# A graph network's first aggregation pass: fp32 rows and weights, or scaled fp16 halves

## What is computed

```python
h = jnp.maximum(_layernorm(x, axis=-1), 0.0)
x = x + _L0_gnn_ref(h, L0_gnn_W, src, dst, edge_weight)
...
Z = jnp.matmul(X, W)
msg = Z[edge_src] * edge_vals[:, None]
agg = jax.ops.segment_sum(msg, edge_dst, num_segments=X.shape[0])
return jax.nn.relu(agg)
```

## Time and profile before

| | us |
|---|---|
| median of 3 runs (2910.2 to 2920.01) | 2912.24 |
| the profiled execution | 2933.06 |
| its span in the trace | 2931.8 |

### The profile page before, as it was taken

The page is one execution under the profiler, slowest core; times in us unless marked ns, Lnnn a source line. Parts: engine busy times, 40 slices in busy tenths (PEclk is TensorE's granted clock), DMA queues, the critical chain, the costliest instruction groups (busy, mean ns, idle before and its releaser), DMA issues.

```text
span 2931.8 us, 38669 instructions
## 1 busy us (share of the span) xinstructions
PE 2508.7 (86%) x9907; PEld 1397.3 (48%) x9907; DVE 1824.4 (62%) x4596; ACT 614.6 (21%) x1144; POOL 872.4 (30%) x900
## 2 busy tenths in 40 slices
PE   7888878868878888999989999998898598888886
PEld 5534444433333223666556556564787443333332
DVE  7765669668567775657333443334887387776666
ACT  4654420000046563000000000001665100000000
POOL 0366665666600000000000000000001466666665
PEclk9889998978976787999999999998999699999899
DMA  6685664555625444344711121111545466776665
GB/s 163 177 236 169 179 179 139 159 164 165 180 42 108 62 63 71 94 110 113 202 46 54 57 58 54 54 32 55 152 121 137 136 189 202 206 233 190 195 191 170
DMA packets 157069, 389.13 MB, mean 133 GB/s; under 512 B 44859, under 2 KB 46260, under 8 KB 156881
## 3 DMA queue, kind: packets, MB, share of 16 engines
q0 software_dynamic: 72400, 232.34, 27.6%
q1 hardware_dynamic: 83798, 153.04, 21.0%
q10 hardware_dynamic: 683, 1.28, 0.2%
HBM read 333.81 MB, written 52.72 MB: 132 GB/s over the span
## 4 chain that ended last, share of the span: by engine, by line
PE 56%; DVE 21%; issue 10%; DMA 6%; another core or an unknown queue 3%; POOL 3%; ACT 1%; SPq 1%; DVEq 0%; ACTq 0%
PE banks L2013 15%; PE banks L1876 15%; PE banks L1842 7%; PE banks L2007 7%; PE banks L2190 4%; DMA ring<-edge_counts 3%; POOL ring L2347 2%; DVE sel L1134 2%; DMA ring<-table,src_t 2%; DVE spare L1061 1%; DVE spare L1059 1%; PE banks L1831 1%; DVE rstd L898 1%; PE banks L2093 1%
## 5 line engine op out<-in xcount | busy, mean ns | idle before, releaser
L1876 PE MATMUL banks<-ring,sel 128*125 128x512 f32 x1682 | 893.1, 659 | 159.5 <-issue 98.4
L1876 PEld LDWEIGHTS banks<-ring,sel 128*125 128x125 f32 x1682 | 287.6, 199 | 476.7 <-issue 473.5
L2292 POOL DMA_INDIRECT ring<-table,src_t x440 | 435.1, 989 | 263.1 <-PE banks L1876 109.1
L2326 POOL DMA_INDIRECT x<-table,src_t x25 | 24.2, 966 | 1461.9 <-DMA x<-src_digits 1447.2
L2347 POOL DMA_INDIRECT ring<-table,src_t x401 | 385.7, 962 | 221.9 <-issue 94.3
L2013 PE MATMUL banks<-acc,ring 125*125 125x512 f16 x1900 | 438.2, 381 | 8.1 <-DVE ring L1262 6.6
L2013 PEld LDWEIGHTS banks<-acc,ring 125*125 125x125 f16 x1900 | 257.1, 137 | 161.9 <-issue 28.9
L1613 DVE TENSOR_TENSOR ring<-ring,banks 128x512 f32<-128x512 f32 x388 | 255.2, 684 | 121.7 <-DMA ring<-table,src_t 98.4
L2007 PE MATMUL banks<-spare 128*125 128x450 f16 x590 | 262.4, 508 | 52.8 <-DVE spare L1061 25.0
L1842 PE MATMUL banks<-wh,hTh 128*125 128x512 f32 x300 | 140.0, 467 | 71.0 <-DVE hTl L914 32.2
L2007 PEld LDWEIGHTS banks<-spare 128*125 128x125 f16 x590 | 92.5, 157 | 223.1 <-issue 221.3
(11 more groups left out here) (411 smaller groups left out, 3132.9 us busy)
## 6 DMA issues: line engine op xcount, KB each, us to landing
ring<-edge_counts SPq DMA_DIRECT2D x35, 683.6 KB
edge_counts<-big SPq DMA_DIRECT2D x175, 97.7 KB
ring<-table,src_t POOLq DMA_INDIRECT x841
sel<-edge_counts SPq DMA_DIRECT2D x11, 683.6 KB
acc<-dst_places SPq DMA_DIRECT2D x28, 256.0 KB
x<-dst_places SPq DMA_DIRECT2D x27, 256.0 KB
acc<-src_digits SPq DMA_DIRECT2D x28, 224.0 KB
x<-src_digits SPq DMA_DIRECT2D x27, 224.0 KB
```

Of the source, the lines that this page charges most:

```text
L1876: last = P.matmul(to, sel[:, n % SELS, :], rows, start=False, stop=True, skip_group_check=True)
L2292: G.indirect_dma_start(out=ring[:, i % RING, :], out_offset=None, in_=table[0][:, :], in_offset=bass.IndirectOffsetOnAxis(ap=src_t[:, i:i ...
```

## The change

`table[0]` becomes fp16 of twice the width: a row's high half, and the rest behind it, 2048 bytes as before. Both are scaled by a power of two, so that they fit fp16. The bound for it comes from the squares of W0 (ScalarE, one `Square` over 2048 columns; TensorE sums them over partitions; VectorE makes the powers in `row_scale`, turn 4). Each tile's product is now taken out twice: ScalarE writes the high half (`z_high`), VectorE the rest (`rows_rest(n - 6)`, behind `rows_low(n - 3)`), and this counts `pj_out`. VectorE's loop has one turn more.

The edge weights get a power of two of their own, from their maximum (VectorE in `step_tables`, TensorE at turns `TABLES_AT`, now 15, and `PEAK_AT`), and are split into two fp16 halves `w16`. A selection is made by one `scalar_tensor_tensor` for both halves, 2x125 columns of fp16 (`sel16`). A step is three fp16 matmuls: high weight by high row, high weight by rest, rest of the weight by high row. ScalarE undoes both scales as it takes a tile out. `zbuf` is replaced by `z_halves_at`, the same room as fp16; the counts of `below` that are waited for later move up by two.

```diff
@@ -111,7 +111,7 @@
     LATE = 4
-    TABLES_AT = 14
+    TABLES_AT, PEAK_AT, SCALES_AT = 15, 17, 300
     DEG_FROM = 46
...
@@ -615,6 +624,41 @@
+            def powers(n):
...
+            def row_scale():
+                V.wait_ge(w0_bound, 2)
+                own.mark(V.tensor_scalar(out=bound[:, 0:1], in0=bank[1][:, 0:1], scalar1=Z_NORM * Z_NORM, scalar2=1e-30, op0=ALU.mult, op1=ALU.max))
+                V.wait_ge(v_own, own.n)
...
+                powers(0)
+                V.tensor_copy(bound[:, 0:1], down[:, 0:1]).then_inc(w0_bound, 1)
+            def weight_scale():
+                V.wait_ge(below, 3)
+                own.mark(V.tensor_scalar(out=bound[:, 1:2], in0=bank[2][:, 128:129], scalar1=1e-30, scalar2=None, op0=ALU.max))
...
+                powers(1)
+                own.mark(V.tensor_tensor(unscale, up[:, 0:1], up[:, 1:2], ALU.mult))
+            def rows_rest(t):
+                V.wait_ge(z_high, t + 1)
+                V.scalar_tensor_tensor(out=z_halves_at(t)[:, D:2 * D], in0=bank[6 + t % 2][0:TN, :], scalar=down[0:TN, 0:1],
+                                       in1=z_halves_at(t)[:, 0:D], op0=ALU.mult, op1=ALU.subtract).then_inc(pj_out, 1)
+
             def iota_row(layer):
@@ -666,6 +710,13 @@
                 V.tensor_copy(dst_f.rearrange("p (c e) -> p c e", c=EC), ed[:, :, 1, :]).then_inc(consts, 1)
+                own.mark(V.memset(squares[:, 1:2], 0.0))
+                own.mark(V.scalar_tensor_tensor(out=dst_junk.rearrange("p (c e) -> p c e", c=EC), in0=edf[:, :, 2, :], scalar=-1.0,
+                                                in1=edf[:, :, 2, :], op0=ALU.mult, op1=ALU.max))
+                V.wait_ge(v_own, own.n)
+                own.mark(V.tensor_reduce(squares[0:EP, 1:2], dst_junk, axis=AX.X, op=ALU.max))
+                V.wait_ge(v_own, own.n)
+                yield
                 V.wait_ge(consts, 8)
@@ -698,6 +749,7 @@
                 V.wait_ge(below, 1)
+                V.tensor_reduce(peak, bank[2][0:1, 0:128], axis=AX.X, op=ALU.max).then_inc(below, 1)
                 own.mark(V.tensor_tensor(thr[:, :], bank[0][:, 0:TILES - 1], tile_f[:, :], ALU.add))
@@ -751,6 +803,7 @@
                 yield
+                weight_scale()
                 yield
@@ -767,7 +820,11 @@
                 V.tensor_copy(dl_t[:, :], bank[1][:, 0:STEPS]).then_inc(tables, 1)
-                V.tensor_copy(w_t[:, :], bank[2][:, 0:STEPS]).then_inc(tables, 1)
+                own.mark(V.tensor_scalar(out=scaled_w, in0=bank[2][:, 0:STEPS], scalar1=down[:, 1:2], scalar2=None, op0=ALU.mult))
+                V.wait_ge(v_own, own.n)
+                own.mark(V.tensor_copy(w16[:, :, 0], scaled_w))
+                V.wait_ge(v_own, own.n)
+                V.tensor_tensor(w16[:, :, 1], scaled_w, w16[:, :, 0], ALU.subtract).then_inc(tables, 1)
                 V.tensor_copy(tile_row[:, :], bank[3][0:1, 0:STEPS]).then_inc(tables, 1)
@@ -783,7 +840,7 @@
             beside = step_tables()
-            for n in range(TILES + 5):
+            for n in range(TILES + 6):
                 if 0 <= n - 1 < TILES:
@@ -792,6 +849,10 @@
                     rows_low(n - 3)
+                if n == 4:
+                    row_scale()
+                if 0 <= n - 6 < TILES:
+                    rows_rest(n - 6)
                 if n > 1:
...
@@ -1131,8 +1192,8 @@
                     V.wait_ge(stepped, step_value(i - SELS))
-                V.tensor_scalar(out=sel[:, i % SELS, :], in0=node_iota[:, :], scalar1=dl_t[:, i:i + 1],
-                                scalar2=w_t[:, i:i + 1], op0=ALU.is_equal, op1=ALU.mult).then_inc(sel_ok, 1)
+                V.scalar_tensor_tensor(out=sel16[:, i % SELS, :, :], in0=node_iota[:, None, :].to_broadcast([CE, 2, TN]), scalar=dl_t[:, i:i + 1],
+                                       in1=w16[:, i, :, None].to_broadcast([CE, 2, TN]), op0=ALU.is_equal, op1=ALU.mult).then_inc(sel_ok, 1)
                 if i == BEHIND - 1:
...
@@ -1736,6 +1797,7 @@
                     split_high(raw_w0)
+                    A.activation(square_junk, raw_w0.rearrange("p k d -> p (k d)"), ACT.Square, accum_out=squares[:, 0:1]).then_inc(w0_bound, 1)
                 t = n
@@ -1744,7 +1806,9 @@
                         wait_stored(A, TABLE_N + t - 3)
-                    A.copy(zbuf(t), bank[6 + t % 2][0:TN, :]).then_inc(pj_out, 1)
+                    if t == 0:
+                        A.wait_ge(w0_bound, 3)
+                    A.activation(z_halves_at(t)[:, 0:D], bank[6 + t % 2][0:TN, :], ACT.Copy, scale=down[0:TN, 0:1]).then_inc(z_high, 1)
@@ -1872,9 +1936,12 @@
                 to = tiles[0:TN, bass.ds(b, 1), :].rearrange("p a d -> p (a d)")
-                rows = ring[:, r, :] if layer < LAST else rows_at(i)
-                last = P.matmul(to, sel[:, n % SELS, :], rows, start=False, stop=True, skip_group_check=True)
-                if layer == LAST:
+                if layer < LAST:
+                    for a, half in ((0, 0), (0, 1), (1, 0)):
+                        last = P.matmul(to, sel16[:, n % SELS, a, :], ring16[:, r, half * D:(half + 1) * D], start=False, stop=True,
+                                        skip_group_check=True)
+                else:
+                    last = P.matmul(to, sel[:, n % SELS, :], rows_at(i), start=False, stop=True, skip_group_check=True)
                     if i % XB == 0:
@@ -1889,6 +1956,8 @@
                     if t == 0:
+                        P.wait_ge(w0_bound, 1)
+                        P.matmul(bank[1][:, 0:1], ones[:, :], squares[:, 0:1], start=True, stop=True).then_inc(w0_bound, 1)
                         P.wait_ge(w_lo, KB)
@@ -1901,7 +1970,11 @@
                     P.wait_ge(counted, TILES - 1)
+                    P.transpose(bank[2][0:1, 0:128], squares[:, 1:2], ident[:, :])
                     P.matmul(bank[0][:, 0:TILES - 1], ones[0:EP, :], cnt[:, :], start=True, stop=True).then_inc(below, 1)
+                if n == PEAK_AT:
+                    P.wait_ge(below, 2)
+                    P.matmul(bank[2][:, 128:129], ones[0:1, :], peak, start=True, stop=True).then_inc(below, 1)
                 if n == TURNED_AT:
...
```

More of the change, by code:

```diff
@@ L152, in build @@
         edge_rows = nc.dram_tensor("edge_rows", (CHUNKS, 3 * CE), I32, kind="Internal").ap()
-        table = [nc.dram_tensor(f"table{n}", (N, D), F32, kind="Internal").ap() for n in range(2)]
+        table = [nc.dram_tensor(f"table{n}", (N, D) if n else (N, 2 * D), F32 if n else F16, kind="Internal").ap() for n in range(2)]
         counts_dram = nc.dram_tensor("edge_counts", (N, TILES * TN), F16, kind="Internal").ap()
@@ L245, in hbuf, with z_halves_at @@
             return stage[0:TN, n % 2 * D:(n % 2 + 1) * D]
-        def zbuf(n):
-            return stage[0:TN, (2 + n % 3) * D:(3 + n % 3) * D]
+        def z_halves_at(n):
+            return stage[0:TN, (2 + n % 3) * D:(3 + n % 3) * D].bitcast(F16)
         raw_w = big[:, 4 * FW:4 * FW + KB * D].rearrange("p (k d) -> p k d", k=KB)
@@ L275, in build @@
         group_bias = score_room[:, 1:GROUPS]
+        bound, exponent, down, up = (score_room[:, SCALES_AT + 2 * n:SCALES_AT + 2 * n + 2] for n in range(4))
+        unscale = score_room[:, SCALES_AT + 8:SCALES_AT + 9]
+        peak = score_room[0:1, SCALES_AT + 9:SCALES_AT + 10]
+        exponent = exponent.bitcast(I32)
+        scaled_w = flat_stage[:, 0:STEPS]
         key_names = score_room[:, 0:KEY_W // 2].bitcast(F16)
         low_names = score_room[:, KEY_W // 2:KEY_W // 2 + (TN + 1) // 2].bitcast(F16)[:, 0:TN]
-        assert KEY_W // 2 + (TN + 1) // 2 <= 2 * TILES * H and BSTEPS + GROUPS <= 2 * STEPS and BSTEPS <= TILES * DEN_W
+        assert KEY_W // 2 + (TN + 1) // 2 <= SCALES_AT and SCALES_AT + 10 <= 2 * TILES * H and BSTEPS + GROUPS <= 2 * STEPS and BSTEPS <= TILES * DEN_W
         unit16 = w_t[0:TN, 0:(TN + 1) // 2].bitcast(F16)[:, 0:TN]
@@ L439, in build @@
         below = signal("below")
+        w0_bound, z_high = signal("w0_bound"), signal("z_high")
         step_no = signal("step_no")
@@ L616, in rows_low @@
                     V.tensor_tensor(low, b, high, ALU.subtract).then_inc(pj_lo, 1)
+            def powers(n):
+                own.mark(V.tensor_scalar(out=down[:, n:n + 1].bitcast(I32), in0=exponent[:, n:n + 1], scalar1=-float(1 << 23),
+                                         scalar2=float(268 << 23), op0=ALU.mult, op1=ALU.add))
+                own.mark(V.tensor_scalar(out=up[:, n:n + 1].bitcast(I32), in0=exponent[:, n:n + 1], scalar1=float(1 << 23),
+                                         scalar2=-float(14 << 23), op0=ALU.mult, op1=ALU.add))
+                V.wait_ge(v_own, own.n)
@@ new lines, in row_scale @@
+            def row_scale():
+                V.wait_ge(w0_bound, 2)
+                own.mark(V.tensor_scalar(out=bound[:, 0:1], in0=bank[1][:, 0:1], scalar1=Z_NORM * Z_NORM, scalar2=1e-30, op0=ALU.mult, op1=ALU.max))
+                V.wait_ge(v_own, own.n)
```

(22 more changed lines are left out.)

13 lines of the change are left out of this document (10 added, 3 removed).

## The result

The changed kernel took 3002.76 us (median of 4 runs, 2998.61 to 3002.97), the kernel before 2911.22 us (4 runs beside it): 1.0293 times as long, 95% interval 1.0271 to 1.0314. That is 91 us more, where +36 was forecast, and outside the range of 2900 to 2990. The profiled execution took 2998.61 us, its span is 2997.3.

A forecast was written before the change was run, and what follows sets the result against it. TensorE was taken to pace the first stage, with TensorE, POOL and VectorE taking turns in the pass. First stage +73 us and pass -37 us net +36: span 2968, time 2948 us, range 2900 to 2990.

The forecast's parts named there:

- First stage, +73: Projection of 25 tiles of rows: 47 + 2 + 2.1 + 22 us longer, +73 us (51 to 88).
- The serial order: First stage: transposes, both splits and the rest run one behind the other, 5.6 us a tile for 3.23, +47 us.
- 22 forecast: First stage: TensorE's clock falls after 7/12 of 22 pauses, 1.7 us each, +22 us (0 to 37).
- The two periods with tables: First stage: VectorE's sums on the tables stand between a wait for TensorE and the next split, +2 us.
- The clock holds: Rival, first stage: the clock stays full through the pauses; net +14 us, 2926 us; chance 0.16.
- the order doesn't bind: Rival, first stage: the reading of the waits is wrong and the rest hides; -33 us, 2879 us; chance 0.06.
- Selection: VectorE in the pass: the two-half selection costs 0.11 us more a step, 48 us, most beside other work.
- fp16 products: TensorE in the pass: three products 0.216 us apart, 0.65 us a step for 0.88, 101 us of TensorE less.
- The pass, -37: First gathering pass of 440 steps: gets 37 us shorter, from an upper bound of 81 us of POOL's waits on TensorE.
- GpSimd's wait for TensorE well under 109 us: Sign in the pass: POOL's waits for TensorE, 109.1 us in the kernel before, were to fall well below that.
- VectorE takes TensorE's place: Rival, pass: TensorE waits longer for VectorE's split, pass returns only 5 us; +68 us, 2980 us; chance 0.15.
- POOL alone bounds: Rival, pass: all 81 us of POOL's wait return and the first stage's clock holds; -30 us, 2882 us; chance 0.11.

The follow-up runs named there:

- one product a step and the cheap selection: Changed kernel with one fp16 product a step in place of three and the old fp32 tensor_scalar selection, edge weights left out: 1.0261, pass 704.2 us.
- the exchanges of selections: Changed kernel with the old fp32 selection: 1.0268, pass 695.8 us; kernel before with the new two-half fp16 selection: 1.0004, pass 698.1 us.
- one swap of two lines: Changed kernel with rows_rest(n - 6) issued ahead of rows_low(n - 3) on VectorE in the first stage: 1.0072, first gather at 130.3 us.

## Why the prediction was wrong

*First stage, +73, measured +78: right in the mechanism and in its two large terms.* The serial order was to give 5.6 us a tile; where the clock held it is 5.52. 16 periods of 7.08 cost 25 us more (22 forecast; 1.56 us each for 1.7, in 16 of the pauses for 7/12 of 22). The two periods with tables, 9.28 and 7.87, are 6.1 above two of 5.52 (2 forecast, the one term well off), the end from the last tile's start to the first gather 10.0 us for 7.3 (+2.7, forecast 2.1). The rule of the Trainium skill (TensorE: Matmul & The Clock Gate, section Why this matters for your kernels), that only longer pauses lower the clock, disagrees with the 16 longer periods after pauses of about 2 us, and with their going when the pause was filled. "The clock holds" and "the order doesn't bind" are out.

*Selection: right.* 0.472 us for 0.359, +0.113 where I took 0.11. By start to start it is 0.387 for 0.254, +0.133; the estimate of 0.195 from the page VectorE: DVE Perf Modes of the Trainium skill, section Mode 2×_2P, is above both. The 60 ns that the prediction allowed for a scalar read from a column stand in no run; 472 is 53 above its 419, and what they are isn't shown.

*fp16 products: right.* They start 0.216 us apart in the pass where the clock is full, not the 0.131 of the Trainium skill (TensorE: Matmul & The Clock Gate, section Back-to-back issue gap).

*The pass, -37, measured -1 (or +3.5 by the gathers): the step that failed.* The prediction took "POOL's waits on TensorE, less the 0.30 that every gather has", 81 us of the 109.1 of the earlier trace rows, for time that faster products can return, and 37 of them for returned. The row names the engine whose signal ended the wait, and not what that engine was doing: in 39 of the 54 late gathers the awaited product had long ended, and its signal was held back. 46 us are left that end with a product, and those didn't come back either: in the changed kernel 42 us of this kind are still there, and with one product a step and the cheap selection 75. TensorE too is stopped by late signals, as at 252 us; how many of the 46 us come of that isn't shown. The prediction never looked up when the awaited step had ended. A look would have cut its upper bound from 81 to about 46 us; a return of 0, which is what the runs show, puts the whole at +73, near 2985. What the prediction named as a sign, GpSimd's wait for TensorE well under 109 us, came out at 93.8. The term for the gathers themselves was missing altogether: they are 22 us longer in all, which doesn't show in the pass on the slower chips, while on the faster one the pass is 25 us longer.

*The rivals.* "VectorE takes TensorE's place" had the nearest price, 2980, by a mechanism that the exchanges of selections refute: with full gathers VectorE's 53 us move nothing. "POOL alone bounds" named the right engine and drew the wrong sum from it: I took its bound for 550 us of work, and all above it for time that TensorE's speed returns. A pass that goes at the pace of the gathers and of late signals has no reason to give anything back.

*The rest.* The two spans differ by 65.5 us and the medians by 91. The profiled execution of before was itself 21 us above its median, and its stages behind the pass took 2120.2 us, those of the changed kernel 2108.7; neither touches them. Of the 91, 78 are the first stage; the other 13 can't be placed, since no traces of the two unedited kernels are known to be from one chip.

## What to carry over

Before an engine's saved time is counted, check a few of the waits attributed to it: when did the awaited instruction end, when was its semaphore updated, and when did the waiting one start? A wait that outlasts its cause by microseconds isn't that engine's work, and no speed of its instructions returned it here. And where a stage moves the release of a buffer to another engine, look at what stands ahead of it in that engine's order: here one swap of two lines was worth 65 of 91 us.

## What the runs showed of the hardware

- A selection of 250 fp16 results on VectorE lengthens the gathers that GpSimd issues beside it: 1026 to 1054 ns in the mean in every kernel that has it, 989 to 1006 in every one that hasn't, whatever TensorE's products are.
- Beside gathers at full rate an engine's semaphore updates can come microseconds late and in bursts: 128 to 215 of 420 steps have an update within 0.1 us of their product's end, against 349 and 393 with half the gathers, and 418 or 419 on one chip with all of them. A waiting gather starts 0.26 us behind the update, late or not.
- The kernel before took 2911 to 2945 us in four comparisons and 2739 in one, on the chip that lacked the stops: 1.46 to 1.54 us a gather against 1.27 to 1.31.
- TensorE with a third of the products spent 547 of 704 us at its lower clock (218 of 697 with all), and its products took 559 ns in the mean for 426: leaving work out made what was left slower.
- Eight filler products of 64 columns, 1.9 us of TensorE in each pause, held the granted clock at 0.97 in the mean of a stage that had 0.82 without.
